# Feed-forward inputs split by GpSimd in rows of tokens and turned by a DMA transfer, with the first feed-forward stages put forward by six steps

## What is computed

```python
x = x + attn(_layernorm(x))      # 16 heads of 64, softmax over 256 keys, projection Wp, bias bp
x = x + ffn(_layernorm(x))

def ffn(x):                      # dim 128, hidden 512
    h = layer_norm(x, ln1_g, ln1_b)
    h = einsum('bsd,hd->bsh', h, ternary_quant(w1)) + b1
    h = gelu(h)
    h = layer_norm(h, ln2_g, ln2_b)
    return einsum('bsh,dh->bsd', h, ternary_quant(w2)) + b2
```

## Time and profile before

| | us |
|---|---|
| three runs | 1027.44, 1027.62, 1029.65 |
| median | 1027.62 |
| the profiled execution's own time | 1027.85 |
| its span in the profile | 1026.1 |
| TensorE busy | 992.7 (97%) |
| VectorE busy | 871.5 (85%) |
| GpSimd busy | 858.0 (84%) |
| ScalarE busy | 721.6 (70%) |

### The profile page before, as it was taken

One profiled execution on the slowest core, in us unless ns is written; L12 is line 12 of the kernel. 1 busy time (PEld: TensorE's weight loads), 2 busy tenths in 40 slices (PEclk: granted clock), 3 DMA queues, 4 the chain that ended last, 5 costly groups with the idle time before them and its releaser, 6 DMA issues.

```text
span 1026.1 us, 39265 instructions
## 1 busy us (share of the span) xinstructions
PE 992.7 (97%) x16045; PEld 783.5 (76%) x16045; DVE 871.5 (85%) x1766; ACT 721.6 (70%) x1104; POOL 858.0 (84%) x834
## 2 busy tenths in 40 slices
PE   4899999999999999999999999999999999989998
PEld 2577778778777877777877777877777777778886
DVE  6898888888788888888888888888888888489998
ACT  4677667767666667666667766766666766679996
POOL 5689999998899999999999999999999997944442
PEclk9999999999999999999999999999999999999999
DMA  5112223222432133223233322223222332221111
GB/s 130 41 31 46 51 43 64 45 51 51 71 51 48 37 68 50 51 51 71 52 51 47 64 57 38 51 46 70 51 51 51 51 51 46 45 52 34 43 32 53
DMA packets 186737, 53.62 MB, mean 52 GB/s; under 512 B 168128, under 2 KB 186304, under 8 KB 186560
## 3 DMA queue, kind: packets, MB, share of 16 engines
q1 hardware_dynamic: 184496, 50.59, 26.4%
q10 hardware_dynamic: 2064, 0.52, 0.2%
HBM read 7.21 MB, written 4.19 MB: 11 GB/s over the span
## 4 chain that ended last, share of the span: by engine, by line
PE 90%; DVE 5%; issue 2%; ACT 2%; POOL 1%; DMA 1%; DVEq 0%; SPq 0%; POOLq 0%; ACTq 0%
PE S L561 15%; PE PV L583 8%; PE S L553 8%; PE PV L585 6%; PE PV L584 6%; PE QK L518 5%; PE M L531 5%; PE QK L520 5%; PE QK L519 5%; PE misc L618 3%; PE misc L619 3%; PE misc L617 3%; PE misc L599 2%; PE misc L598 2%; PE misc L597 2%
## 5 line engine op out<-in xcount | busy, mean ns | idle before, releaser
L996 POOL TENSOR_TENSOR pl<-p 128x1024 f16<-128x1024 f32 x256 | 484.5, 1893 | 65.8 <-ACT p L810 65.3
L810 ACT ACTIVATE p<-S,s_exp 128x1024 f32<-128x1024 f32 x256 | 285.2, 1114 | 123.7 <-PE S L561 123.6
L1163 DVE TENSOR_REDUCE negmax<-M 128x4 f32<-128x1024 f32 x252 | 307.3, 1219 | 50.4 <-PE M L531 48.2
L818 ACT ACTIVATE QKh<-QK 128x512 f16<-128x512 f32 x251 | 149.8, 597 | 134.6 <-PE QK L520 134.4
L583 PEld LDWEIGHTS PV<-V,p 128*128 128x128 bf16 x2048 | 185.2, 98 | 57.5 <-issue 36.6
L583 PE MATMUL PV<-V,p 128*128 128x65 f16 x2048 | 215.8, 194 | 3.7 <-DVE V L1189 2.5
L1183 DVE TENSOR_TENSOR QKl<-QK,QKh 128x512 f16<-128x512 f32 x251 | 172.7, 688 | 52.6 <-ACT QKh L818 52.1
L584 PE MATMUL PV<-V,p 128*128 128x64 f16 x2048 | 213.4, 192 | 0.0
L585 PE MATMUL PV<-V,pl 128*128 128x65 f16 x2048 | 212.6, 194 | 0.0
L584 PEld LDWEIGHTS PV<-V,p 128*128 128x128 bf16 x2048 | 189.2, 98 | 0.0
L585 PEld LDWEIGHTS PV<-V,pl 128*128 128x128 f16 x2048 | 188.8, 97 | 0.0
(11 more groups left out here) (182 smaller groups left out, 2254.8 us busy)
## 6 DMA issues: line engine op xcount, KB each, us to landing
result<-X SPq DMA_DIRECT2D x16, 256.0 KB, 2.3
X<-in_L_attn_query SPq DMA_DIRECT2D x7, 512.0 KB, 4.8
OT<-O SPq DMA_TRANSPOSE x64, 4.4
shift<-negmax SPq DMA_TRANSPOSE x63, 2.3
O<-in_L_attn_Wk ACTq DMA_DIRECT2D x1, 512.0 KB, 5.3
O<-in_L_attn_Wq SPq DMA_DIRECT2D x1, 512.0 KB, 5.6
O<-in_L_attn_Wv SPq DMA_DIRECT2D x1, 512.0 KB, 7.0
w<-in_L_ffn_w SPq DMA_DIRECT2D x2, 256.0 KB, 5.6
```

Source lines behind the costliest of these rows:

```text
L810: e.activation(p32[r][:, :, :, :].rearrange("p i m n -> p (i m n)"), S[:, :], ACT.Exp, scale=s_exp[:, :]).then_inc(s_ex, 1)
L996: e.tensor_tensor(pl[r][:, :, :, :].rearrange("p i m n -> p (i m n)"), p32[r][:, :, :, :].rearrange("p i m n -> p (i m n)"), p_high(r).rea ...
L1163: e.tensor_reduce(dst[:, :, NB * jj:NB * jj + NB], max_bank(p)[:, :].rearrange("p (i t m) -> p i t m", i=2, t=NB), AX.X, ALU.max, negate=T ...
```

## The change

Four things are changed.

1. The inputs y of the first product are no longer transposed by TensorE and split in PSUM. They are split where they are, in rows of tokens, into a tile yp that holds high and low parts side by side: the high part by ScalarE for the first two groups (`f_yhi`) and by GpSimd from the third on, the low part always by GpSimd (`f_ysplit`). One transposing transfer for each group, eight blocks of 128 x 128, issued by SyncE (`turn_y`), puts both parts into yT. `turn_y(g)` waits for the low part and, from the third group on, for the first products of group g - 2, whose buffer it writes.
2. FFN_LEAD goes from 5 to 11, so that u = t - 245. `f_y` keeps its place at u = i; the stages behind it get lags that are greater by four (first product and GELU at i + 10, `f_zT` at i + 11, second product at i + 13, sum at i + 17). Against attention's steps, `f_y` moves forward by six steps and the rest by two. `f_bias` moves from i to i + 10.
3. Banks: first products go to M instead of S, the transposed a to S instead of QK and PV, second products to QK and PV instead of the misc banks. The waits for the last users of these banks change with them.
4. The instructions `f_yT` (64) and `f_ylo` (16), and 14 of the 16 `f_yhi`, are gone.

The diff without the waits for the first use of each bank:

```diff
-FFN_LEAD, TAIL = 5, 9
+FFN_LEAD, TAIL = 11, 9
-L_YT, L_HID, L_ZT, L_OUT, L_SUM = 1, 6, 7, 9, 13
+L_BIAS, L_HID, L_ZT, L_OUT, L_SUM = 10, 10, 11, 13, 17
+Y_BY_ACT = 2
...
-        yT_bank, pre_bank, z_bank = (M[:, 0:512], M[:, 512:1024]), (S[:, 0:512], S[:, 512:1024]), (QK, PV)
+        pre_bank, z_bank, f_banks = (M[:, 0:512], M[:, 512:1024]), (S[:, 0:512], S[:, 512:1024]), (QK, PV)
...
+            def turn_y(g):
+                e.wait_ge(s_ylo, g + 1)
+                if g >= 2:
+                    e.wait_ge(s_pre, FG * (g - 1))
+                e.dma_start_transpose(yT[g % 2][:, :, :, :].rearrange("p k s n -> p (k s) n"),
+                                      yp[g % 2][:, :, :, :].rearrange("p k s d -> p (k s d)")).then_inc(yt_in[g % 2], 16)
...
+                if u is not None and u % FG == FG - 1 and u < NT:
+                    turn_y(u // FG)
                 if u is not None and 0 <= u - L_SUM < NT and (u - L_SUM) % STORE == STORE - 1:
                     store(u - L_SUM)
...
             def f_hidden(i):
                 g, k = divmod(i, FG)
-                e.wait_ge(s_ylo, g + 1)
+                if k == 0:
+                    e.wait_ge(yt_in[g % 2], 16 * (g // 2 + 1))
...
-            def f_yT(i):
-                g, k = divmod(i, FG)
-                e.wait_ge(s_y1, i + 1)
...
-                e.transpose(yT_bank[g % 2][:, k * P:(k + 1) * P], y[g % 2][:, k, :], ident[:, :]).then_inc(s_yt, 1)
...
             def f_yhi(g):
-                e.activation(yTh[g % 2][:, :, :], yT_bank[g % 2].rearrange("p (k n) -> p k n", k=FG),
-                             ACT.Copy).then_inc(s_yhi, 1)
+                e.wait_ge(s_y1, FG * g + FG)
+                e.wait_ge(s_y0, 2)
+                e.activation(yp[g][:, :, 0, :], y[g][:, :, :], ACT.Copy).then_inc(s_yhi, 1)
...
+            def f_ysplit(g):
+                if g >= Y_BY_ACT:
+                    e.wait_ge(s_y1, FG * g + FG)
+                    e.wait_ge(yt_in[g % 2], 16 * (g // 2))
+                    e.tensor_copy(yp[g % 2][:, :, 0, :], y[g % 2][:, :, :]).then_inc(s_yhi, 1)
+                e.wait_ge(s_yhi, g + 1)
+                e.tensor_tensor(yp[g % 2][:, :, 1, :], y[g % 2][:, :, :], yp[g % 2][:, :, 0, :],
+                                ALU.subtract).then_inc(s_ylo, 1)
...
-                if 0 <= u < NT:
-                    f_bias(u)
+                if 0 <= u - L_BIAS < NT:
+                    f_bias(u - L_BIAS)
...
-            def f_ylo(g):
-                e.wait_ge(s_yhi, g + 1)
```

More of the change, by code:

```diff
@@ L276, in layer @@
         y = [sb(f"y{i}", [P, FG, D]) for i in range(2)]
-        yTh = [sb(f"yTh{i}", [P, FG, P], F16) for i in range(2)]
-        yTl = [sb(f"yTl{i}", [P, FG, P], F16) for i in range(2)]
+        yp = [sb(f"yp{i}", [P, FG, 2, D], F16) for i in range(2)]
+        yT = [sb(f"yT{i}", [P, FG, 2, P], F16) for i in range(2)]
         a = [sb(f"a{i}", [P, F]) for i in range(A_RING)]
@@ L294, in layer @@
         xt_in, shift_in = sem("s_x_transposed"), sem("s_shift_transposed")
+        yt_in = [sem(f"s_ffn_y_transposed{i}") for i in range(2)]
         stored = sem("s_store")
@@ L315, in layer @@
         s_st1, s_mv1, s_ve1, s_r1, s_mr1, s_nm1 = (sem(f"s_{n}") for n in ("st1", "mv1", "ve1", "root1", "mean_root1", "negmean1"))
-        s_y0, s_y1, s_yt, s_yhi, s_ylo = (sem(f"s_ffn_{n}") for n in ("y0", "y", "yT", "yT_hi", "yT_lo"))
+        s_y0, s_y1, s_yhi, s_ylo = (sem(f"s_ffn_{n}") for n in ("y0", "y", "y_hi", "y_lo"))
         s_pre, s_a, s_st2, s_mv2, s_ve2, s_r2, s_rs2 = (
@@ L343, in f_bank @@
         def f_bank(i):
-            return misc_banks[1 - i // FG % 2]
+            return f_banks[i // FG % 2]
         def qk_bank(p):
@@ L687, in f_hidden @@
                 g, k = divmod(i, FG)
-                e.wait_ge(s_ylo, g + 1)
+                if k == 0:
+                    e.wait_ge(yt_in[g % 2], 16 * (g // 2 + 1))
                 if i == 0:
-                    e.wait_ge(s_ex, NP)
+                    e.wait_ge(s_mx, NP)
                 if i >= 2:
                     e.wait_ge(s_a, i - 1)
[L693 to L696, removed]
+                o, hi, lo = pre_bank[i % 2], yT[g % 2][:, k, 0, :], yT[g % 2][:, k, 1, :]
+                e.matmul(o, hi, T1h[:, :], start=True, stop=False)
+                e.matmul(o, hi, T1l[:, :], start=False, stop=False)
+                e.matmul(o, lo, T1h[:, :], start=False, stop=True).then_inc(s_pre, 1)
             def f_zT(i):
@@ L700, in f_zT @@
                 if i == 0:
-                    e.wait_ge(s_qklo, NP)
-                if i == 1:
-                    e.wait_ge(s_o, NP)
+                    e.wait_ge(s_ex, NP)
                 if i >= 2:
@@ L712, in f_out @@
                 e.wait_ge(s_zlo, i + 1)
-                if k == 0 and g < 2:
-                    e.wait_ge(*misc_done(*misc_lists[1 - g][-1]))
+                if i == 0:
+                    e.wait_ge(s_qklo, NP)
+                elif i == FG:
+                    e.wait_ge(s_o, NP)
                 elif k == 0:
@@ L755, in pe_program @@
                     e.wait_ge(s_lo, LO_AT["T2l"])
-                for lag, fn in ((L_HID, f_hidden), (L_ZT, f_zT), (L_OUT, f_out), (L_YT, f_yT)):
+                for lag, fn in ((L_HID, f_hidden), (L_ZT, f_zT), (L_OUT, f_out)):
                     if 0 <= u - lag < NT:
@@ L947, in act_program @@
                         fn(u - lag)
-                if u % FG == 0 and FG <= u <= NT:
-                    f_yhi(u // FG - 1)
+                if u % FG == FG - 1 and u // FG < Y_BY_ACT:
+                    f_yhi(u // FG)
         def pool_program(e):
@@ L1093, in pool_program @@
                     continue
-                if u == 0:
+                if u % FG == FG - 1 and u < NT:
+                    f_ysplit(u // FG)
+                if u == L_BIAS:
                     e.wait_ge(s_w, W_AT["bias2"])
-                if 0 <= u < NT:
-                    f_bias(u)
+                if 0 <= u - L_BIAS < NT:
+                    f_bias(u - L_BIAS)
                 if (u - L_ZT) % FG == FG - 1 and 0 <= u - L_ZT < NT:
@@ L1370, in dve_program @@
                         e.memset(y[i][:, :, D - 1:D], 1.0).then_inc(s_y0, 1)
-                if u % FG == 1 and FG < u <= NT + 1:
-                    f_ylo(u // FG - 1)
                 for lag, fn in ((L_ZT, f_stats), (L_SUM, f_sum), (L_ZT, f_variance), (L_ZT, f_zlo)):
```

10 lines of the change are left out of this document (1 added, 9 removed).

## The result

The changed kernel takes 1034.37 us in the median (1032.83 to 1036.29), the kernel before, run in turn with it, 1028.3. The ratio is **1.0058, with a 95% interval from 1.0046 to 1.0070**: slower by 6 us. The direction is the forecast's; the time lies 4.1 us above the 1030.3 that were forecast, and 0.9 above the range. The profiled execution took 1032.83, with a span of 1030.7. It was the shortest of its four.

A forecast was written before the change was run, and what follows sets the result against it. TensorE was taken to bound. Tile 8 at 920.2 us, the old remainder less 6.2 saved, gave 1026.4; clock 2.4 and 1.75 outside the span gave 1030.55, a median of 1030.3 us. Own range 1029.5 to 1033.5, overall 1024.0 to 1033.5.

The forecast's parts named there:

- The saving: From tile 8's first product on, 51 transposes of y leave TensorE, 1.877 to 1.755 us a step: 6.2 us.
- the copy: GpSimd's added copy per group of y: taken as 1.0 us, between 0.58 and 3.2.
- the transfer: A group's transposing transfer of y holds SyncE 1.34 us, lands in 2.4 to 4.4, and is hidden in the steady part.
- GpSimd's room: Steady part, four steps of 7.02 us: after 3.4 busy and a 1.16 subtraction, the copy has under 2.4 us.
- this rival: GpSimd becomes the bound through a copy of 3.2 us, giving about 1043 us, slower; chance 0.05.
- The hand-over, step by step: t = 256 to 263: TensorE idles 0.9, 2.5, 2.5 and 5.3 us; tile 8's first product comes at 920.2.
- the hand-overs don't bite: Rival: weighted(254) and (255) wait for nothing, giving 1025.3 us, or 1023.6 if the clock holds too; chance 0.17.
- the change does nothing of weight: Rival: savings and gaps are both smaller than thought and cancel, giving 1027.6 us; chance 0.06.
- Up to t = 254 ... I take the sum as zero: Before the hand-over: instructions added and removed balance, 0.5 us either way; the last shifts land some 2 us later.
- The clock: TensorE slows behind its idle gaps: 1.7 us behind the 5.3 us gap, 0.7 behind the two of 2.5 us.
- the clock holds: Rival: the walk is right but the gaps cost only themselves, 1027.9 us, no change; chance 0.24.
- The sum: 1026.4 us plus clock 2.4 gives a span of 1028.8; 1.75 outside it gives 1030.55, less 0.23 for the median.

The follow-up runs named there:

- f3: Changed kernel with only the first transfer of y moved behind the last shifts on SyncE: 1032.45 us, 1.0036 of the kernel before.
- k1: Changed kernel plus twenty matmuls without use in TensorE's last gap, ahead of the second projection piece of t = 263: 1032.35 us, 1.0041 of the kernel before.
- f4: Changed kernel plus matmuls without use in three TensorE gaps, nine at t = 257, nine at t = 258, twenty at t = 263: 1030.53 us, 1.0023 of before.
- f2: Changed kernel with all sixteen transfers of y two steps later in SyncE's list: 1023.97 us, 0.9956 of the kernel before.
- k4: Changed kernel with stages from first product on two steps later, transfers of y five and GpSimd's copies three steps later: 1024.01 us, 0.9960 of before.
- h2: Changed kernel with FFN_LEAD 9, transfers of y three steps later on SyncE and GpSimd's copies one step later: 1020.80 us, 0.9929 of before.

## Why the prediction was wrong, point by point

**The saving, the copy, the transfer, GpSimd's room: right.** 5.8 us came where 6.2 were forecast. The copy takes 0.61 us (row L1066 above) and its pitch to the next instruction is 0.69; I had 1.0. The Trainium skill (GPSIMD Engine Reference, section 3.1) has 769 ns for one input of 512 elements; the trace decides. All of these are far from the 2.4 from which GpSimd would have bound, so that this rival is out too. A group's transfer holds SyncE for 1.34 us (914.62 to 915.96), as forecast, and lands in 3.1 in the median, between the 2.4 and 4.4 of the forecast.

**The hand-over, step by step: right as a walk.** 0.79, 2.34, 2.34 and 4.90 us of waits stood where 0.9, 2.5, 2.5 and 5.3 were forecast, ended by what was named. GpSimd's order, turn_y(3) at 914.62 and the half at 915.96 were as walked. The rival "the hand-overs don't bite" is out for this kernel, and so is "the change does nothing of weight". The first of them was also mis-summed: with the hand-overs' gaps their 0.7 for the clock goes too, so that its two times are 1024.6 and 1022.9, not 1025.3 and 1023.6.

**"Up to t = 254 ... I take the sum as zero": the step that failed.** I had seen that turn_y(0) stands ahead of the last shifts, and wrote that these "land some 2 us later, just ahead of the scores of t = 252 that need them". Before, they landed at 877.49, 2.1 us ahead of those scores (879.59), so a delay of 2 us would just have fitted. It was 3.4: they were issued 1.4 us later (876.60 against 875.19) and took 4.3 us to land, not 2.3, at 880.90. The scores waited 1.90, of which 1.4 is new, and f3 prices the sentence at **1.9 us** by its median.

The Trainium skill (DMA: Bandwidth & Descriptors, Queues, rings and completion order) says that each DMA engine takes its descriptors in ring order, and that a transfer's semaphore step lands only after the earlier writes of that engine. The trace is in keeping with it, for y landed at 878.38 and the shifts at 880.90. But y had landed 2.5 us before them, so that this order does not by itself show why they took 4.3 us.

**The clock: right mechanism, term too small.** I charged 1.7 and 0.7. By the medians the fall behind the last gap cost 2.0 (k1) and the one behind the hand-overs 1.8 (f4 less k1), together **3.8 for 2.4**; the sum is clear of noise, the division is not. The term for the hand-overs was halved because I took "less than half lies on the chain". But TensorE's stretch 903 to 907 was at 0.62, which held tile 7 up by 1.1 us even in the profiled execution, the shortest. The rival "the clock holds" is out.

**The sum.** By the medians, shifts 1.9 and clock 1.4 make 3.3 of the 4.1 us, and 0.8 is not assigned. The profiled execution can be followed term by term. The forecast for it was 1030.55, and it took 1032.83, 2.3 us more. Of these, 1.2 are there when weighted(253) starts (891.08 against 889.89), which is the wait for the shifts. From there to tile 8 the clock cost 0.5 more than charged (1.1 and 1.8 against 0.7 and 1.7), and the last half landed 0.2 sooner than walked. The pace of 1.763 makes 0.4, in part the clock again, since the first step took 1.91; and 0.4 lies outside the span (2.1 us against 1.75). The rest of the 4.1, 1.8 us, is the place of this execution among the others: I took the profiled one to be 0.23 above the median, and it was 1.5 below. This execution alone would have been inside the range. That the four spread over 3.5 us, and that the clock cost the other three more (their granted clock was lower), was in no term.

**What I never asked** is what else could hide these waits. The forecast treats them as the price of the change. f2 shows that 10 us of the changed kernel's time was the place of one call in SyncE's loop.

## What to carry to other kernels

When a transfer is added to a queue, list every transfer that it now precedes, and give each the landing time behind it and the time at which its reader wants it; "just ahead of" is no number. Then try the new transfer one or two steps later, as far as its own reader allows: here that turned 0.6% slower into 0.4% faster. And where TensorE bounds, price a wait of it with the slower clock behind it too, about 2 us for each fall here; but don't count on its removal in full, since the next late transfer takes up what is won.

## What the runs showed of the hardware

A transposing transfer lands at nearly the same time whenever no packet of an instruction queue is in flight with it. These are the queues that the page calls `instruction`, q8 and q14. Over the 14 traces, with none of their packets between issue and landing, one block took 2.29 to 2.32 us (375 transfers), eight blocks 3.06 to 3.27 (116) and sixteen 4.23 to 4.49 (358), with and without other transposes around them. Every longer landing, up to 4.3, 5.9 and 6.2, has at least one such packet beside it, though many transfers with one are not late. The DMA view of k4 from 902.3 to 908.5, around the last half of O, and of f2 from 908.7 to 913:

```profile
q8 instruction: 1, 0.02, 1.0%
q14 instruction: 1, 0.01, 0.3%
...
OT<-O SPq DMA_TRANSPOSE x1, 6.1
```

```profile
q1 hardware_dynamic: 2080, 0.52, 64.2%
...
OT<-O SPq DMA_TRANSPOSE x1, 4.3
```

The shifts of the changed kernel fit in. In all four profiles that have the transfer of y ahead of them, a packet of q8 is in flight and they take 3.8 to 4.3 us; in the other ten none is, and they take 2.3. So the order on SyncE moved the shifts into the packet's time. That the packet is the cause is argued from these pairs and not shown, for no run moves it.

The clock fell behind stretches in which TensorE was far from idle. In the changed kernel it was busy 3.31 of 5 us with the clock at 1.00, and then came the fall to 0.62; in h2 a stretch that was a little less busy, 3.16 of 5, was followed by none. The changed kernel:

```profile
897.00:902.00 5.00, 3.31 (x55) 2.79 (x55) 1.39 (x6) 1.38 (x3) 2.82 (x5) 1.00 0.00 0
```

h2, with a clock of 1.00 from 900 to 904 as well:

```profile
895.00:900.00 5.00, 3.16 (x26) 1.81 (x23) 3.10 (x9) 4.02 (x9) 4.67 (x10) 1.00 0.75 140
```

The forecast of the falls was made from two stretches, 1.52 and 2.41 busy of 4; the one at 903 has 3.64 busy itself, with the two gaps of 2.34 ahead of it. In these rows the busy share of one stretch doesn't tell whether the clock falls behind it.
